# Transposing DMAs for the rounded tokens, products and bit matrices of a gated attention and feed-forward layer, a VectorE addition of bias and maximum, and a new order

## The chip, the cores and the metric

The kernel runs on one core of one Trainium2 chip. The metric is the device time of one execution in microseconds (us); the number quoted for a kernel is the median of its runs.

## What is computed

The input is 8 batches of 512 tokens with 256 features. Cut to what matters:

```python
x = x + tanh(g_xattn) * xattn(layernorm(x), ctx)      # windowed attention-free layer + MLP
x = x + tanh(g_ffn) * ffn(layernorm(x))               # ternary weights, 8-bit activations

def xattn(x, pos):                       # T=512, D=256, H=1024
    emb = x + pos
    q, k, v = emb @ wq + bq, emb @ wk + bk, emb @ wv + bv
    ek = exp(k - max(k, axis=1)); ew = exp(w - max(w, axis=1))    # w = pos_bias within 64 tokens
    y = sigmoid(q) * (ew @ (ek * v)) / (ew @ ek)
    a = layer_norm(y @ wo + bo + emb, gamma, beta)
    return layer_norm(relu(a @ w1 + b1) @ w2 + b2 + a, gamma, beta)

def act_quant(x):  scale = 127 / max(abs(x)) per token; return round(x * scale) / scale
def weight_quant(w): scale = 1 / mean(abs(w)); return clip(round(w * scale), -1, 1) / scale
def bitlinear(x, w): return act_quant(x) @ weight_quant(w).T
def ffn(x): return bitlinear(silu(bitlinear(x, w_gate)) * bitlinear(x, w_up), w_down)
```

## The kernel before

**Tiling.** A batch is four tiles of 128 tokens. Matrix products in single precision are made of three matmuls each (upper by upper, upper by lower, lower by upper half of the operands, helper `product` of the matmuls, L2342). The matmuls of the ternary feed-forward part (`gate`, `up`, `down`) are one bf16 matmul each, since rounded tokens (up to 127) and weights (-1, 0, 1) fit in bf16.

**Stages of a batch.** `emb_rows` (transposes of x + pos), `keys_T` and `key_max`/`max_row` (maximum of the keys over the tokens), `queries`, `keys_values` (k and v of a tile in one bank of 512 columns, `kv`), `attend` and `attend_far`, `project`, `n1_rows`, `hidden`, `feed_forward`, then the ternary part. Eight batches overlap: while batch b is in its keys and attention, batch b-1 is in `hidden` and `feed_forward`, and batch b-3 (later b-2) is in the ternary part.

**Keys and values.** The bias of k less the maximum, and the bias of v, are split in an upper and a lower row (`bias_parts` on VectorE, L1529 to L1534) and added by a matmul of a matrix of ones with `bias_row` (L2393), ahead of the six matmuls of the tile. ScalarE takes `exp` of k in place (L783) and copies v out (`copy_values`, L789); VectorE multiplies (`weighted`, L1541); ScalarE and VectorE split the result (`e_upper` L796, `e_lower` L1546).

**Rounding and transposing.** Tokens are rounded by adding a large number (`token_quantise`, L834), so that the rounded value lies in the low half of each 32-bit word. TensorE transposes these halves as f16 into PSUM (`xq_rows`, L2480, four transposes for two tiles), and ScalarE turns them into bf16 (`xq_columns`, L853). The products of a tile, 128 x 1024, go the same way: `product` on VectorE (L1625), its absolute maximum and scale (`product_scale`, L1631 to L1643), rounding on GpSimd for even tiles (L492) and on ScalarE for odd ones (L867), eight transposes (`hq_rows`, L2507), `hq_columns` on ScalarE (L874), `down` (L2515), `output` on VectorE (L1649). The three weight matrices, rounded once at the start, go through `bit_rows` (L2339, 16 transposes each) and `bit_columns` (L747).

**What sets the order.** Each engine has a list of steps written out by hand in its block, and does them strictly in that order. A step begins with its waits on semaphores. SyncE's list holds the DMAs, in order too: an entry that waits holds back those behind it. The table `BANK` says in which of the eight PSUM banks each step of each batch writes, and `bank_wait` lets TensorE wait for the last reader of the bank's earlier content.

Of the kernel before, what the change touches and what calls it, by code (L numbers as in the profile page):

```python
# [23 lines left out]
LIFT = ROUND + 16896.0  # L24
LIFT_SCALE, LIFT_BASE = 512.0, 1536.0
# [12 lines left out]
    ("embT", 0): (4, 3, 0, 5, 0, 3, 5, 1), ("embT", 1): (5, 6, 1, 3, 3, 5, 1, 3), ("kT", 0): (4, 5, 6, 5, 0, 3, 5, 1),  # L38
# [3 lines left out]
    ("num", 0): (1, 1, 4, 7, 6, 6, 6, 3), ("den", 0): (2, 5, 3, 3, 5, 1, 3, 5), ("num", 1): (0, 6, 1, 4, 0, 3, 5, 0),  # L42
# [5 lines left out]
    ("xqT", 0): (2, 5, 1, 2, 4, 2, 7, 3), ("xqT", 1): (2, 0, 3, 5, 1, 2, 1, 6), ("gate", 0): (4, 4, 0, 2, 4, 2, 6, 2),  # L48
    ("up", 0): (0, 6, 6, 6, 6, 2, 0, 6), ("hqT", 0): (2, 0, 3, 5, 3, 6, 0, 0), ("down", 0): (4, 0, 3, 5, 3, 6, 0, 0),
    ("gate", 1): (4, 4, 0, 2, 4, 2, 6, 2), ("up", 1): (4, 4, 0, 2, 4, 4, 0, 0), ("hqT", 1): (5, 3, 5, 1, 1, 7, 2, 1),  # L50
# [3 lines left out]
    ("down", 3): (0, 3, 5, 1, 6, 6, 3, 0)}  # L54
PAIRED = ("gate", "up")
EWT_BANKS = (0, 1, 2, 3)
TOTAL_BANKS = (0, 3, 7)
BIT_BANKS = ((5, 4), (7, 3), (2, 5))
B1_BANK = 1

# [11 lines left out]
def flamingo_layer(nc, x, ctx_in, g_xattn, g_ffn, wq, bq, wk, bk, wv, bv, wo, bo, pos_bias, gamma, beta,  # L72
                   w1, b1, w2, b2, w_gate, w_up, w_down, out):
    with ExitStack() as stack:
# [594 lines left out]
        def _(act):  # L669
# [2468 lines left out]
```

## Time and profile before

| | |
|---|---|
| median of 3 runs | 554.49 us (552.69 to 555.13) |
| profiled execution, its own time | 555.27 us |
| span of the profile | 553.5 us |
| TensorE busy | 505.9 us, 91% |
| VectorE busy | 426.3 us, 77% |
| ScalarE busy | 380.0 us, 69% |
| GpSimd busy | 245.2 us, 44% |

The profile calls the engines PE (TensorE matmul), PEld (weight load), DVE (VectorE), ACT (ScalarE), POOL (GpSimd) and SP (SyncE; SPq are the DMAs that it issues). Lines as L2507 are lines of the kernel. The rows hold only the operation, so a helper's line stands for all who call it: all three-part products are L2348. A matmul's duration in a row includes its way through the array; matmuls overlap, so that the time that one costs is the distance of its start to the next one's start.

### The profile page before, as it was taken

How to read it: one execution, taken by the hardware profiler on the slowest of the kernel's cores; microseconds unless marked ns; L12 is line 12 of the kernel's file. 1: busy time of each engine (PE TensorE's matmuls, PEld its weight loads, DVE VectorE, ACT ScalarE, POOL GpSimd, SP SyncE). 2: the span in 40 equal slices, each digit the busy share in tenths (PEclk: the TensorE clock that was granted, in tenths of full speed). 3: DMA queues.
4: the chain of work that ended last, by engine and by line, in shares of the span. 5: the costliest groups of instructions: out<-in, count | busy, mean ns of one | idle time of the engine just before them, and what ended most of it. 6: DMA issues, size and time to landing. Idle time of an engine off the chain costs nothing.

```text
span 553.5 us, 10265 instructions
## 1 busy us (share of the span) xinstructions
PE 505.9 (91%) x3270; PEld 412.3 (74%) x3270; DVE 426.3 (77%) x974; ACT 380.0 (69%) x627; POOL 245.2 (44%) x384
## 2 busy tenths in 40 slices
PE   0389999999999999999999999999999999999474
PEld 0378788988877887788877897788778877877332
DVE  3883997766899769976999679975988688858564
ACT  2667866648576877697667877677658866877474
POOL 3654106229512870359223951277114922547410
PEclk9998999999999999999999999999999999999588
DMA  7835001101200211011200120012001100010101
GB/s 258 259 92 190 2 0 39 40 1 38 77 2 1 78 40 39 1 40 38 78 1 12 67 76 2 1 46 70 1 2 39 40 0 1 14 62 5 37 3 38
DMA packets 25608, 25.31 MB, mean 46 GB/s; under 512 B 3538, under 2 KB 24532, under 8 KB 25556
## 3 DMA queue, kind: packets, MB, share of 16 engines
q1 hardware_dynamic: 24720, 24.65, 14.0%
q8 instruction: 28, 0.46, 0.4%
q14 instruction: 24, 0.20, 0.1%
q10 hardware_dynamic: 836, 0.01, 0.1%
HBM read 20.46 MB, written 4.19 MB: 45 GB/s over the span
## 4 chain that ended last, share of the span: by engine, by line
PE 82%; DVE 6%; issue 3%; ACT 3%; POOL 2%; DMA 2%; SPq 1%; ACTq 1%; POOLq 0%; DVEq 0%
PE ps L2348 53%; PE ps L2488 10%; PE ps L2515 5%; PE ps L2507 3%; PE ps L2417 3%; PE ps L2393 1%; PE ps L2365 1%; PE ps L2442 1%; ACT hqT L874 1%; PE ps L2425 1%; DVE ps L1555 1%; DMA bkv_row<-in_L_xattn_bv_dram 1%; PE ps L2356 1%; DMA x_in<-in_x_dram 1%; PE ps L2318 1%
## 5 line engine op out<-in xcount | busy, mean ns | idle before, releaser
L436 POOL TENSOR_TENSOR mv<-mv,cols 128x2 f32<-128x2 f32 x64 | 12.6, 197 | 169.1 <-DVE mv L1504 169.1
L822 ACT ACTIVATE h_hi<-ps,cols 128x512 fp32r<-128x512 f32 x64 | 44.0, 690 | 51.6 <-PE ps L2348 51.3
L2348 PE MATMUL ps<-w_hi,h_hi 128*128 128x256 f32 x256 | 74.9, 292 | 0.0
L2348 PE MATMUL ps<-w_hi,h_lo 128*128 128x256 f32 x256 | 71.4, 279 | 0.0
L2348 PE MATMUL ps<-w_lo,h_hi 128*128 128x256 f32 x256 | 71.4, 279 | 0.0
L874 ACT ACTIVATE hqT<-ps,cols 128x1024 bf16<-128x1024 f16 x32 | 35.6, 1113 | 32.0 <-PE ps L2507 31.9
L1555 DVE RECIPROCAL ps<-ps 128x512 f32<-128x512 f32 x16 | 53.7, 3359 | 4.3 <-PE ps L2425 4.3
L2348 PE MATMUL ps<-n1T_hi,w_hi 128*128 128x512 f32 x128 | 52.2, 408 | 1.1 <-DVE y_lo L1572 1.0
L1590 DVE TENSOR_TENSOR h_lo<-ps,h_hi 128x512 fp32r<-128x512 f32 x64 | 42.7, 684 | 12.6 <-ACT ps L827 12.3
L2348 PE MATMUL ps<-n1T_hi,w_lo 128*128 128x512 f32 x128 | 50.6, 395 | 0.0
L2348 PE MATMUL ps<-n1T_lo,w_hi 128*128 128x512 f32 x128 | 50.5, 394 | 0.0
L2348 PEld LDWEIGHTS ps<-w_hi,h_hi 128*128 128x128 f32 x256 | 48.1, 188 | 1.4
L2348 PEld LDWEIGHTS ps<-w_lo,h_hi 128*128 128x128 f32 x256 | 48.2, 188 | 0.8
L2348 PEld LDWEIGHTS ps<-w_hi,h_lo 128*128 128x128 f32 x256 | 48.1, 188 | 0.0
L1625 DVE TENSOR_TENSOR work<-work,ps 128x1024 f32<-128x1024 f32 x32 | 38.7, 1210 | 9.4 <-ACT work L862 6.2
L439 POOL TENSOR_TENSOR rstd<-mv,cols 128x2 f32<-128x2 f32 x64 | 44.5, 696 | 0.0
L862 ACT ACTIVATE work<-ps,cols 128x1024 f32<-128x1024 f32 x32 | 35.6, 1113 | 11.6 <-PE ps L2488 10.8
L2515 PE MATMUL ps<-wdT,hqT 128*128 128x256 bf16 x256 | 35.9, 286 | 7.9 <-ACT hqT L874 7.9
L827 ACT ACTIVATE ps<-ps,cols 128x512 f32<-128x512 f32 x64 | 42.1, 658 | 0.0
L1496 DVE BATCH_NORM_STATS2 st<-work 128x6 f32<-128x256 f32 x96 | 36.3, 414 | 3.8 <-POOL work L486 3.5
L1631 DVE TENSOR_REDUCE cols<-work 128x1 f32<-128x1024 f32 x32 | 38.7, 1210 | 0.4
L2348 PE MATMUL ps<-ew_hi,e_hi 128*128 128x256 f32 x128 | 37.7, 295 | 0.9 <-DVE e_lo L1546 0.7
(180 smaller groups left out, 1508.2 us busy)
## 6 DMA issues: line engine op xcount, KB each, us to landing
x_in<-in_x_dram SPq DMA_DIRECT2D x16, 256.0 KB, 2.9
emb<-in_ctx_dram SPq DMA_DIRECT2D x16, 256.0 KB, 3.0
work<-in_x_dram SPq DMA_DIRECT2D x8, 512.0 KB, 3.7
out_dram<-work SPq DMA_DIRECT2D x16, 256.0 KB, 2.1
work<-in_L_xattn_w_dram SPq DMA_DIRECT2D x2, 1024.0 KB, 10.0
place_c<-in_L_xattn_pos_bias_dram SPq DMA_DIRECT2D x1, 1024.0 KB, 7.4
work<-in_L_ffn_w_gate_dram SPq DMA_DIRECT2D x1, 1024.0 KB, 5.7
work<-in_L_ffn_w_up_dram SPq DMA_DIRECT2D x1, 1024.0 KB, 6.2
```

The source lines that it names most:

```text
L439: pool.tensor_tensor(rstd[:, n, c], mv[:, n, c, 1], minus_half[:, c], ALU.pow).then_inc(rstd_ok[n].sem, 1)
L822: nc.scalar.activation(h_hi[:, m % RING, :], bank(b, "h", m), ACT.Relu, bias=b1_col[:, m:m + 1]).then_inc(h_hi_ok.sem, 1)
L827: nc.scalar.activation(bank(b, "h", m), bank(b, "h", m), ACT.Relu, bias=b1_col[:, m:m + 1]).then_inc(h_relu_ok.sem, 1)
L874: nc.scalar.activation(hqT[:], bank_h(b, "hqT", t).rearrange("p (k n) -> p k n", n=P), ACT.Identity, bias=unlift_col, scale=LIFT_SCALE).th ...
L1496: nc.vector.bn_stats(st6[:, n, t, :], src[:, t, :]).then_inc(stats[n].sem, 1)
L1555: nc.vector.reciprocal(bank(b, "den", h), bank(b, "den", h)).then_inc(rden_ok.sem, 1)
L1590: nc.vector.tensor_tensor(h_lo[:, m % RING, :], bank(b, "h", m), h_hi[:, m % RING, :], ALU.subtract).then_inc(h_lo_ok.sem, 1)
L1625: nc.vector.tensor_tensor(prod[t % 2].rearrange("p (a n) -> p a n", a=2), sg.rearrange("p (a n) -> p a n", a=2), bank_pair(b, "up", t), AL ...
L1631: nc.vector.tensor_reduce(hm[:, t:t + 1], prod[t % 2], AX.X, ALU.max, apply_absolute_value=True).then_inc(hm_ok.sem, 1)
L2348: last = nc.tensor.matmul(dst, lhsT, rhs, start=(i == 0 and not begun), stop=(i == n - 1 and ends))
L2488: last = nc.tensor.matmul(dst[:, c, :], xqT[:, k, t * P:(t + 1) * P], w[:, k, c * T:(c + 1) * T], start=(k == 0), stop=(k == ND - 1))
L2515: last = nc.tensor.matmul(bank(b, "down", t)[:, 0:D], hqT[:, k, :], wdT[:, k, :], start=(k == 0), stop=(k == NH - 1))
```

## The change

**Transposes.** `xq_rows`, `hq_rows` and `bit_rows` leave TensorE's list. In their place stand DMAs that transpose 2-byte elements from SBUF to SBUF, issued by SyncE. Their source has to be bf16, so ScalarE first writes the rounded values as bf16 (`xq_whole`, `hq_whole`, `bit_whole`); the steps `xq_columns`, `hq_columns` and `bit_columns` go. `hqT` has two buffers in place of one. `gate`, `up` and `down` read their weights from blocks of 128 columns with a gap between.

**Keys and values.** `max_row` has the row of maxima in all partitions; VectorE subtracts it from the bias in one operation (`bias`) and adds the whole bias to each tile of k and v in one (`add_bias`), which also moves them to SBUF. The ones matmul, `bias_parts` and `copy_values` go, and `keys_values` no longer waits for the maximum.

**Order.** All lists, and the table of banks, are new. Start: the weights of keys and values are loaded second and split first. End: the maximum of the last batch's first tokens stands ahead of `output(6, 3)` on VectorE, and `output(7, 0)` ahead of `product(7, 3)`.

```diff
+            def xq_rows(b, p):
+                wait(sp, xq_ok, b, p + 1)
+                wait(sp, g_ps, b, 2 * p - 2)
+                wait(sp, u_ps, b, 2 * p - 2)
+                sp.dma_start_transpose(xqT[:, 2 * p:2 * p + 2, :, :], half(xq, p)).then_inc(xqT_ok[p].sem, 16)
+            def hq_rows(b, t):
+                wait(sp, hq_ok, b, t + 1)
+                sp.wait_ge(bitT_ok, 48)
+                wait(sp, d_ps, b, t - 1)
+                sp.dma_start_transpose(hqT[t % 2], hq[t % 2]).then_inc(hqT_ok[t % 2].sem, 16)
...
-                nc.scalar.activation(v_f[:, t % 2, :], bank(b, "kv", t)[:, D:2 * D], ACT.Copy).then_inc(v_ok.sem, 1)
+                nc.scalar.activation(bank(b, "kv", t)[:, 0:D], kv_f[:, t % 2, 0:D], ACT.Exp).then_inc(ek_ok.sem, 1)
...
+            def xq_whole(b, p):
+                wait(act, xr_ok, b, p + 1)
+                wait(act, xqT_ok[p], b - 1, 16)
+                nc.scalar.activation(half(xq, p), half(n3, p), ACT.Identity, bias=unlift_col).then_inc(xq_ok.sem, 1)
...
+            def hq_whole(b, t):
+                c, n = rounded_of(t)
+                wait(act, c, b, n)
+                act.wait_ge(bit_ok, 3)
+                wait(act, hqT_ok[t % 2], b, 16 * (t // 2))
+                nc.scalar.activation(hq[t % 2], prod[t % 2], ACT.Identity, bias=unlift_col).then_inc(hq_ok.sem, 1)
...
+            def bias(b):
+                wait(dve, mrow_ps, b, 1)
+                wait(dve, kvb_ok, b, 0)
+                nc.vector.tensor_tensor(bias_all[:, 0:D], bk_all[:], bank(b, "mx")[:, 0:D], ALU.subtract).then_inc(bias_ok.sem, 1)
+            def add_bias(b, t):
+                wait(dve, kv_ps, b, t + 1)
+                wait(dve, bias_ok, b, 1)
+                wait(dve, ekv_ok, b, t - 1)
+                nc.vector.tensor_tensor(kv_f[:, t % 2, :], bank(b, "kv", t), bias_all[:], ALU.add).then_inc(kvb_ok.sem, 1)
...
-                nc.tensor.matmul(dst, ones_r[:], bias_row[:], start=True, stop=False)
...
-                        last = nc.tensor.matmul(dst[:, c, :], xqT[:, k, t * P:(t + 1) * P], w[:, k, c * T:(c + 1) * T],
+                        last = nc.tensor.matmul(dst[:, c, :].rearrange("p (j n) -> p j n", n=P), xqT[:, t, k, :], w[:].rearrange("p (j k) n -> p j k n", k=ND)[:, 4 * c:4 * c + 4, k, :],
...
-                    last = nc.tensor.transpose(bank_h(b, "hqT", t)[:, k * P:(k + 1) * P], hq_h[t % 2][:, k * P:(k + 1) * P], ident_h[:])
```

TensorE's order between the second tile's `down` of batch 2 and the keys and values of batch 5; before:

```order
L2348 MATMUL ps<-wkv_hi,embT_lo 128x512
L2515 MATMUL ps<-wdT,hqT 128x256 x8
L2507 MATMUL ps<-ident_h,work 128x128 x8
L2393 MATMUL ps<-bias_row,ones_r 128x512
L2348 MATMUL ps<-wkv_hi,embT_hi 128x512
```

and now:

```order
L2365 MATMUL ps<-wkv_hi,embT_lo 128x512
L2512 MATMUL ps<-wdT,w_bit 128x256 x8
L2365 MATMUL ps<-wkv_hi,embT_hi 128x512
L2365 MATMUL ps<-wkv_lo,embT_hi 128x512
L2365 MATMUL ps<-wkv_hi,embT_lo 128x512
```

The eight transposes and the bias matmul between `down` and the tile's six matmuls are gone; `w_bit` holds the transposed products.

VectorE's order at the first product of batch 2 (`product`, bias of batch 5, `product_scale`, `first_residual` of batch 4), before:

```order
L1625 TENSOR_TENSOR work<-work,ps 128x1024
L1529 TENSOR_TENSOR ps<-bkv_row,ps 1x256
L1532 CAST bias_row<-ps 1x256
L1534 TENSOR_TENSOR bias_row<-ps,bias_row 1x256
L1631 TENSOR_REDUCE cols<-work 128x1
L1635 TENSOR_SCALAR cols<-cols 128x1
```

and now:

```order
L1628 TENSOR_TENSOR work<-work,ps 128x1024
L1531 TENSOR_TENSOR bias_all<-bk_all,ps 128x256
L1634 TENSOR_REDUCE cols<-work 128x1
L1638 TENSOR_SCALAR cols<-cols 128x1
L1641 RECIPROCAL cols<-cols 128x1
```

Three operations on one row have become one on 128 partitions, ahead of the maximum of the product.

SyncE's DMAs from batch 5's context to the reload of batch 4's x (`x_in` and `emb` inputs, `out_dram` stores, `work<-in_x_dram` the reload), before:

```order
L282 DMA emb<-in_ctx_1024_dram 128x2x256 x2
L276 DMA x_in<-in_x_dram 128x2x256 x2
L291 DMA out_dram<-work 128x2x256 x2
L287 DMA work<-in_x_dram 128x4x256
L282 DMA emb<-in_ctx_1024_dram 128x2x256 x2
```

and now:

```order
L267 DMA emb<-in_ctx_1024_dram 128x2x256 x2
L290 DMA_TRANSPOSE xqT<-xq 128x4x128 x2
L261 DMA x_in<-in_x_dram 128x2x256 x2
L297 DMA_TRANSPOSE w_bit<-place_c 128x8x128 x3
L276 DMA out_dram<-work 128x2x256
L297 DMA_TRANSPOSE w_bit<-place_c 128x8x128
L276 DMA out_dram<-work 128x2x256
```

Six transposing DMAs of a batch stand in the same queue as its loads and stores: the loads of x wait behind those of the tokens, the stores behind those of the products.

## Rows read from the trace of the kernel before

**Rows 1.** The page: busy time of each engine, share of the span, instructions.

```profile
PE 505.9 (91%) x3270; PEld 412.3 (74%) x3270; DVE 426.3 (77%) x974; ACT 380.0 (69%) x627; POOL 245.2 (44%) x384
```

**Rows 2.** Windows: one batch, the full stretch, the end; busy us, granted clock.

```profile
236.60:297.00 60.40, 60.33 (x399) 49.31 (x398) 49.76 (x117) 44.35 (x76) 28.94 (x46) 1.00 0.12 36
120.20:506.10 385.90, 384.12 (x2526) 314.69 (x2524) 311.29 (x719) 280.20 (x474) 184.56 (x283) 1.00 0.10 31
506.10:553.50 47.40, 28.69 (x178) 15.79 (x176) 28.44 (x74) 26.99 (x36) 13.55 (x26) 0.77 0.07 23
```

**Rows 3.** Timeline of TensorE: start us, us; eight transposes, bias matmul, next matmuls.

```profile
302.48 0.61 PE L2507 MATMUL ps<-ident_h,work 128*128 128x128 f16 x8
302.90 0.48 PE L2393 MATMUL ps<-bias_row,ones_r 128*128 128x512 f32 x1
303.21 0.39 PE L2348 MATMUL ps<-wkv_hi,embT_hi 128*128 128x512 f32 x1
```

**Rows 4.** Chain that ended last, in order of time: start us, us, what.

```profile
463.44 1.41 PE ps L2348 x12
...
465.31 0.86 PE ps L2488 x4
...
504.17 0.46 PE ps L2507 x8
504.63 0.22 PE ps L2480 x4
```

**Rows 5.** Timeline of TensorE: transposes of the first weight matrix.

```profile
41.06 1.87 PE L2339 MATMUL ps<-ident_h,work 128*128 128x128 f16 x16
42.68 0.78 PE L2393 MATMUL ps<-bias_row,ones_r 128*128 128x512 f32 x1
```

**Rows 6.** Groups of VectorE: xcount | busy us, mean ns | idle before.

```profile
L1590 DVE TENSOR_TENSOR h_lo<-ps,h_hi 128x512 fp32r<-128x512 f32 x64 | 42.7, 684 | 12.6 <-ACT ps L827 12.3
...
L1529 DVE TENSOR_TENSOR ps<-bkv_row,ps 1x256 f32<-1x256 f32 x8 | 3.3, 409 | 0.8 <-PE ps L2382 0.8
```

**Rows 7.** Groups of ScalarE, same columns.

```profile
L874 ACT ACTIVATE hqT<-ps,cols 128x1024 bf16<-128x1024 f16 x32 | 35.6, 1113 | 32.0 <-PE ps L2507 31.9
...
L867 ACT ACTIVATE work<-work,cols 128x1024 f32<-128x1024 f32 x16 | 19.8, 1238 | 4.0 <-DVE cols L1640 4.0
```

**Rows 8.** DMA issues: xcount, KB each, median us from issue to landing.

```profile
x_in<-in_x_dram SPq DMA_DIRECT2D x16, 256.0 KB, 2.9
...
out_dram<-work SPq DMA_DIRECT2D x16, 256.0 KB, 2.1
...
vecs<-in_L_xattn_b_dram SPq DMA_DIRECT2D x1, 128.0 KB, 4.8
```

**Rows 9.** Timeline of TensorE: end of first up, eight transposes, first down, batch 2.

```profile
282.00 0.61 PE L2382 MATMUL ps<-ident,cols 128*128 128x128 f32 x4
...
288.05 0.62 PE L2507 MATMUL ps<-ident_h,work 128*128 128x128 f16 x8
...
291.94 1.04 PE L2515 MATMUL ps<-wdT,hqT 128*128 128x256 bf16 x8
```

**Rows 10.** Timeline of GpSimd: rounding of that tile's products.

```profile
286.88 1.11 POOL L492 TENSOR_SCALAR work<-work,cols 128x1024 f32<-128x1024 f32 x1
```

**Rows 11.** Chain, the end: tokens of batch 7, its last tile.

```profile
526.63 0.62 PE ps L2480 x4
...
527.27 0.70 ACT xqT L853
...
528.21 3.44 PE ps L2488 x8
...
547.27 1.12 ACT hqT L874
...
548.53 1.88 PE ps L2515 x8
```

**Rows 12.** Timeline of ScalarE: upper half of the key and value weights.

```profile
28.17 1.05 ACT L683 ACTIVATE wkv_hi<-work 128x1024 fp32r<-128x1024 f32 x1
```

More of the change, by code:

```diff
@@ L1330, in _ @@
             silu(5, 1)
-            hq_columns(5, 0)
+            hq_whole(5, 0)
             normalise_tile(7, 0)
@@ L2268, in _ @@
             tile_stats(7, 2, 3)
-            output(6, 0)
+            product(6, 2)
             mean_variance(7, 2, 1)
-            product(6, 2)
             product_scale(6, 2)
             product(6, 3)
+            output(6, 0)
             output(6, 1)
@@ L2602, in _ @@
             hidden(0, 3)
+            feed_forward(0, 0)
+            feed_forward(0, 1)
+            emb_rows(2, 0)
             hidden(0, 4)
@@ L2605, in _ @@
             hidden(0, 6)
-            hidden(0, 7)
-            feed_forward(0, 0)
-            feed_forward(0, 1)
             feed_forward(0, 2)
             feed_forward(0, 3)
+            hidden(0, 7)
             project(1, 0)
@@ L2660, in _ @@
             attend(2, "num", 1, 3)
+            feed_forward(1, 2)
+            attend_far(2, "den", 0)
+            attend_far(2, "den", 1)
+            attend(2, "num", 0, 1)
+            attend(2, "num", 0, 2)
+            attend(2, "num", 0, 3)
+            attend_far(2, "num", 0)
             attend_far(2, "num", 1)
@@ L2670, in _ @@
             feed_forward(1, 4)
+            feed_forward(1, 5)
+            gate(0, 0)
             keys_T(3, 0)
             keys_T(3, 1)
-            queries(3, 0)
-            gate(0, 0)
-            queries(3, 1)
             up(0, 0)
+            gate(0, 1)
             max_row(3)
-            gate(0, 1)
             project(2, 0)
@@ L2745, in _ @@
             keys_T(4, 1)
-            queries(4, 0)
+            feed_forward(2, 5)
             gate(1, 0)
-            queries(4, 1)
             up(1, 0)
@@ L2818, in _ @@
             keys_T(5, 1)
-            queries(5, 0)
+            feed_forward(3, 5)
             gate(2, 0)
-            queries(5, 1)
             up(2, 0)
@@ L2883, in _ @@
             hidden(4, 5)
+            hidden(4, 6)
             feed_forward(4, 3)
-            hidden(4, 6)
             hidden(4, 7)
             emb_rows(6, 0)
+            project(5, 0)
+            project(5, 1)
+            project(5, 2)
+            project(5, 3)
+            gate(3, 0)
+            up(3, 0)
             emb_rows(6, 1)
@@ L2952, in _ @@
             attend(6, "num", 1, 3)
+            attend_far(6, "den", 0)
+            feed_forward(5, 2)
+            attend_far(6, "den", 1)
+            attend(6, "num", 0, 1)
+            attend(6, "num", 0, 2)
+            attend(6, "num", 0, 3)
+            attend_far(6, "num", 0)
             attend_far(6, "num", 1)
@@ L2956, in _ @@
             hidden(5, 5)
+            hidden(5, 6)
             feed_forward(5, 3)
-            hidden(5, 6)
+            gate(4, 0)
             hidden(5, 7)
+            up(4, 0)
+            gate(4, 1)
+            project(6, 0)
+            gate(4, 2)
+            project(6, 1)
+            project(6, 2)
+            project(6, 3)
+            up(4, 1)
             emb_rows(7, 0)
@@ L2981, in _ @@
             down(4, 0)
+            max_row(7)
             feed_forward(5, 6)
             gate(4, 3)
-            hq_rows(4, 1)
+            queries(7, 0)
+            queries(7, 1)
+            down(4, 1)
             feed_half(5)
```

1797 lines of the change are left out of this document (846 added, 951 removed), and 16 rows, old and new, of the table BANK.

## The prediction

> **What bounds the kernel now.** I read the page's busy times first, then the windows, then the chain of waits. TensorE is busy 91% of the span, VectorE 77%, ScalarE 69% [rows 1]. The windows say where the missing 9% of TensorE is: from 120.2 to 506.1 us it is busy 384.1 of 385.9 us at a granted clock of 1.00, while VectorE is busy 311.3 us in the same stretch [rows 2]. So for 386 us the kernel is as long as TensorE's list, and whatever leaves that list there leaves the time. The other two parts differ: a start of some 68 us, where loads and the first chain set the pace, and an end of 47.4 us, where TensorE is busy 28.7 us at a mean clock of 0.77 [rows 2] and the chain goes from engine to engine. There an operation of TensorE counts only as one link of a chain, and so does what replaces it. The profiled execution took 555.27 us for a span of 553.5 us, 0.8 us above the median; I sum on the span and carry the difference over.
>
> **What leaves TensorE.** A matmul costs the distance to the next start. The bias matmul of 512 columns: its start to the next one's is 0.31 us in the row shown, of which 0.08 us come from the change of type after the transposes, so 0.23 us, and 32 x 0.23 = 7.4 us; all lie ahead of 506 us. Eight transposes of products cost 0.42 us on the timeline [rows 3] and 0.46 us on the chain [rows 4]; 24 of the 32 groups (batches 0 to 5) and the first of batch 6 lie ahead of 506 us: 25 x 0.44 = 11.0 us. Four transposes of tokens cost 0.22 us [rows 4]; 14 of 16 groups lie ahead: 3.1 us. The three weight matrices: the first costs 1.6 us (41.06 to 42.68 us, before the clock rose) [rows 5], the others I count at twice the 0.44 us of eight, 0.9 us each: 3.4 us. Together 24.9 us. Of the single batch that I looked at, 60.4 us long [rows 2], this takes 4 x 0.23 + 4 x 0.44 + 2 x 0.22 = 3.1 us, which makes 57.3 us.
>
> **What VectorE takes over.** `add_bias` moves 128 x 512 from PSUM; the nearest row, a subtraction of that size from PSUM, has 0.684 us, and the three one-row operations that go have 0.41 us each, one like them staying [rows 6]. Per batch 4 x 0.68 - 3 x 0.41 + 0.41 = +1.9 us: VectorE goes from 49.8 us of 60.4 (82%) to 51.7 of 57.3 (90%). What hides it is that VectorE works for other batches ahead of need; TensorE's three `hidden` after the keys and values are its cover. If that cover failed altogether, each of the 4 x 0.68 us would be a stall of TensorE: 2.7 us a batch, 18 us over some 6.5 batches. If it holds, 0. I take 2.5 us in all, near the lower end, since 5.6 us of VectorE's batch stay free. ScalarE loses the copy of v and reads the products from SBUF (1.24 us as its rounding there, against 1.11 us from PSUM) [rows 7]: nearly even, no new bound.
>
> **The transposing DMA, the unknown.** No row shows one. Call L the time from the ready bf16 to the landed transpose of 128 x 1024 (256 KB). The nearest rows are plain DMAs: a store of 256 KB out of SBUF 2.1 us, a load into SBUF 2.9 us, and 4.8 us for a 128 KB one that stood behind others [rows 8]. I take 3 us, by the load of the same size, and keep 2.1 and 5 us as bounds; that transposing could cost more is a rival below. What does the new order leave for L? In the batch shown, `up` of the first tile ends at 282.0 us and its `down` starts at 291.94 us, 9.9 us later [rows 9]; the new list puts both `queries` between (12 matmuls at 0.23 us, 2.8 us) and takes a `feed_forward` (12 matmuls of 256 columns, 1.4 us), one `up` (0.9 us) and the transposes (0.5 us) out [rows 4], so the distance stays at 9.9 us. The rounding ended at 286.88 + 1.11 = 288.0 us, 6.0 us after `up` [rows 10]; with two one-row operations less ahead of it on VectorE it is 5.2 us. `hq_whole` adds 1.24 us and a hand-over 0.1 us: 6.5 us. So 3.4 us are left for L, and by the same count about 3.4 us for the third tile; the second has about 4.4 us, the fourth more than 8. With L = 3 nothing waits. Above 3.4 us each of the first and third tile stalls TensorE by the excess, twice a batch. The tokens' transposes have more than 10 us. Behind a waiting transpose on SyncE stand the loads of x and the stores; x is needed two batches later, so they have room.
>
> **The Trainium skill on this.** The page "VectorE: DVE Perf Modes", section "The three transpose paths", gives 1309 ns for one 128 x 128 transpose by DMA against 390 ns on TensorE, and advises TensorE where PSUM will do. This trace has 0.46 us for eight on TensorE in a row, far below that figure, and nothing for the DMA. The page "Advanced Engine Details and Errata", section "X-Bar Transpose (TRN2)", says that they are as fast as regular DMAs, which is the assumption of the sum above; the first, taken eight times in a row, would be L = 10.5 us, an estimate from that page, and by it the kernel would be far slower.
>
> **Start.** The split of the key and value weights (1.05 us) stands at 28.17 us between the two halves of the embedding on ScalarE, with TensorE waiting for the second [rows 12]; it moves ahead into idle time: -1.0 us. The order of the loads shifts the rest by up to 1 us either way.
>
> **End.** Three places get longer by the DMA. Tokens of batch 7: now 0.62 us of transposes and 0.70 us of columns, 1.6 us from 526.63 to 528.21 us [rows 11]; then some 0.7 us for `xq_whole` plus L plus 0.1 us = 3.8 us: +2.2. The last tile: rounding ended at 546.03 us (544.80 + 1.24, the mean of its row), `down` started at 548.53 us, 2.5 us [rows 7, 11]; then 1.24 + 3 + 0.1 = 4.3 us: +1.8. `output(7, 0)` now stands ahead of `product(7, 3)` on VectorE and waits for a first tile that is later by L: about +1.5. Against this, the maximum of batch 7's first tokens no longer stands behind `output(6, 3)`: -1.1. End: +4.4 us, and 3 us more for each us of L.
>
> **The sum.** 553.5 - 24.9 - 1.0 + 2.5 + 4.4 = 534.5 us of span; with the 1.8 us around it 536.3, less 0.8 us to the median: 535.5 us.
>
> **The rivals.** (a) L between 3.4 and 4.5 us, partly uncovered. At 4 us: 0.6 us x 2 x 6.5 batches = 8 us in the full stretch, 3 us at the end: 546.5 us. For it: a transposing DMA can hardly be quicker than a plain one. Against: the plain ones here are below 3.4 us. (b) Slower than before: the transposes are the bound. At L = 5 us it is 1.6 x 2 x 6.5 = 21 us and 6 us at the end: 562 us. The place is the first and third `down` of each batch; it decides from L = 4.5 us on, where 1.1 x 13 + 4.5 = 19 us cancel the forecast's gain of 19 us. By the skill's 1309 ns eight times over, this case would be the one, with 7.1 x 13 + 22 = 114 us, some 650 us. For it: many small pieces make a DMA slow, as the 4.8 us of 128 KB hint. (c) VectorE becomes the bound: it is 90% full, and its list waits at other places than before. At the full 18 us in place of my 2.5 us: 551 us. Against: even now it waits over 10 us a batch without holding TensorE up. (d) The gapped weights of `gate` and `up` stream slower; no row shows such an operand. Double time would be 256 x 0.22 = 56 us; nothing speaks for it, 2 in 100, kept in (b)'s share.
>
> **Chances.** Forecast (L up to 3.4 us, cover holds) 0.50; (a) 0.20; (c) 0.12; (b) with (d) 0.18. A measurement of this kernel tells about 0.5% (2.8 us) from no change. Faster: 0.50 + 0.20 + half of (c) and a little less = 0.76; same: 0.06, from the edges of (b) and (c); slower 0.18. The low end: L = 2.1 us gives -2.7 at the end, full cover -2.5, the start -1 more: 529; with stalls of TensorE in the first 120 us that a better order could take away, 525 us. The high end is (c) whole and (b) at its mild end, 556 us. Outside lie the rest of (b) and little else, under 2 in 10.
>
> **What would show it.** TensorE's window between two batches' keys and values at 57 to 58 us and still over 99% busy; transposing DMAs landing 2.5 to 3.4 us after issue; VectorE at about 52 us a batch; no wait of a `down` matmul for a DMA in the full stretch, and such waits of 2 us and more at the end. Wrong, if the window is 60 us or more: with idle time ahead of `down` it is (b) or (a); with waits of the attention matmuls for VectorE's lower halves it is (c); with TensorE's `gate` matmuls above 0.22 us apart it is (d).

## The result and the profile after

The changed kernel takes 538.47 us (median of 4 runs, 534.96 to 538.88) against 554.32 us for the kernel before in the same session: a ratio of 0.970, 95% interval 0.966 to 0.975. It is faster by 15.9 us; the forecast was 19. The profiled execution took 538.58 us for a span of 536.8 us, and I compare spans. Two executions of the experiments below, one of 1236.8 us in extra_512 and one of 552.47 us in late_bits, lie apart from the others of their kernels, and the medians given are those of the others.

The page after; engine, busy us, share of the span, instructions, against [rows 1]:

```profile
PE 476.4 (89%) x2870; PEld 386.4 (72%) x2870; DVE 432.5 (81%) x984; ACT 375.3 (70%) x592; POOL 246.3 (46%) x384
```

TensorE's busy time fell by 29.5 us, the span by 16.7: TensorE now idles 12.8 us more. The windows say where. Their columns are the stretch, its length, busy us of PE, PEld, DVE, ACT and POOL, then granted clock, DMA share and GB/s; the fourth row is one batch, from its first `add_bias` to the next batch's, the last is the end:

```profile
0.00:41.50 41.50, 15.68 (x78) 13.99 (x78) 23.45 (x58) 21.85 (x29) 20.82 (x33) 0.88 0.74 218
41.50:122.80 81.30, 74.61 (x447) 64.35 (x447) 62.88 (x129) 48.62 (x78) 27.34 (x46) 0.98 0.24 61
122.80:234.40 111.60, 110.31 (x685) 91.11 (x684) 97.98 (x227) 84.96 (x140) 57.43 (x90) 1.00 0.21 54
234.40:291.85 57.45, 56.44 (x355) 46.54 (x353) 50.94 (x120) 43.88 (x72) 29.16 (x46) 1.00 0.28 61
291.85:353.97 62.12, 60.09 (x367) 49.48 (x365) 54.14 (x128) 45.97 (x74) 29.07 (x46) 0.97 0.24 62
...
486.60:536.80 50.20, 27.25 (x113) 12.13 (x112) 29.68 (x79) 27.41 (x36) 13.52 (x26) 0.68 0.34 69
```

A batch takes 57.45 us against 60.40 [rows 2]. Ahead of the end TensorE's busy time fell by 28.1 us (477.2 us up to 506.1 before, 449.2 up to 486.6 now). Part of this did not come out as time: TensorE idles 5.4 us more in the first 122.8 us (32.5 us against 27.1 before) and 3.2 us more in the stretch behind (4.9 us against 1.8 [rows 2]). The end, behind the last matmul of `feed_forward`, is 50.2 us against 47.4. So -28.1 + 5.4 + 3.2 + 2.8 = -16.7 us.

TensorE's waits from 19 us, behind its first, to the end of the stretch; us in total, times, longest:

```profile
PE ps L2373 <- POOL emb L504: 5.4, 1, 5.4
PE ps L2365 <- DVE embT_lo L1510: 3.2, 1, 3.2
PE ps L2365 <- DVE y_lo L1575: 2.0, 2, 1.7
PE ps L2365 <- DVE e_lo L1549: 1.7, 1, 1.7
PE ps L2382 <- ACT embT_hi L823: 1.6, 2, 1.1
...
PE ps L2512 <- DMA w_bit<-place_c: 0.3, 1, 0.3
```

Two more groups, small ones, recur from batch to batch. In the one batch from 225.92 us (its first `down`) to 283.36 us TensorE waits twice for VectorE, ahead of the transposes of the embedding:

```profile
PE ps L2373 <- DVE h_lo L1593: 0.6, 1, 0.6
PE ps L2373 <- DVE y_lo L1575: 0.3, 1, 0.3
```

`down` waits for a transposing DMA 0.3 us in all before the end, and 14.2 us in the end. What the DMA takes from issue to landing, over the stretch from 120 to 486 us:

```profile
w_bit<-place_c SPq DMA_TRANSPOSE x24, 3.1
xqT<-xq SPq DMA_TRANSPOSE x14, 2.7
```

How close this is, the four tiles of batch 2 show. ScalarE writes the bf16 products (start us, us):

```profile
278.76 1.15 ACT L920 ACTIVATE place_c<-work,cols 128x1024 bf16<-128x1024 f32 x1 [1.35 <-POOL work L549]
285.56 1.14 ACT L920 ACTIVATE place_c<-work,cols 128x1024 bf16<-128x1024 f32 x1
288.81 1.15 ACT L920 ACTIVATE place_c<-work,cols 128x1024 bf16<-128x1024 f32 x1
296.03 1.15 ACT L920 ACTIVATE place_c<-work,cols 128x1024 bf16<-128x1024 f32 x1
```

and TensorE starts the four `down`, never idle before them:

```profile
283.36 0.38 PE L2512 MATMUL ps<-wdT,w_bit 128*128 128x256 bf16 x2
291.07 0.39 PE L2512 MATMUL ps<-wdT,w_bit 128*128 128x256 bf16 x2
293.35 0.39 PE L2512 MATMUL ps<-wdT,w_bit 128*128 128x256 bf16 x2
301.32 0.39 PE L2512 MATMUL ps<-wdT,w_bit 128*128 128x256 bf16 x2
```

From the end of each write to the start of its `down` are 3.4, 4.4, 3.4 and 4.1 us, and the DMA needs 3.1. For the first and the third tile 0.3 us are to spare.

### The profile page after: what moved, and what is told of

The parts are those of the page before. It is cut to its first block, busy times and chain, and to the rows that moved or that the text cites. A ratio compares the mean times of both kernels' runs of the same rounds, so it can differ in the third digit from the quotient of the medians.

```text
span 536.8 us, 9468 instructions
## 1 busy us (share of the span) xinstructions
PE 476.4 (89%) x2870; PEld 386.4 (72%) x2870; DVE 432.5 (81%) x984; ACT 375.3 (70%) x592; POOL 246.3 (46%) x384
## 4 chain that ended last, share of the span: by engine, by line
PE 69%; DVE 14%; DMA 6%; ACT 5%; issue 4%; POOL 1%; SPq 0%; DVEq 0%; ACTq 0%; POOLq 0%
PE ps L2365 47%; PE ps L2493 9%; DVE ps L1558 5%; PE ps L2512 5%; PE ps L2431 3%; DMA work<-in_L_xattn_w_dram 2%; DMA w_bit<-place_c 2%; DVE cols L1634 2%; PE ps L2382 1%; DVE ps L1571 1%; PE ps L2456 1%; PE ps L2373 1%; DVE work L1628 1%; DMA wuT<-w_bit 1%; PE ps L2439 1%
## 5 line engine op out<-in xcount | busy, mean ns | idle before, releaser
L869 ACT ACTIVATE h_hi<-ps,cols 128x512 fp32r<-128x512 f32 x64 | 44.3, 692 | 29.5 <-PE ps L2365 27.5
L2512 PE MATMUL ps<-wdT,w_bit 128*128 128x256 bf16 x256 | 38.3, 300 | 14.5 <-DMA w_bit<-place_c 14.5
L920 ACT ACTIVATE place_c<-work,cols 128x1024 bf16<-128x1024 f32 x32 | 36.7, 1147 | 14.7 <-POOL work L549 14.1
L2512 PEld LDWEIGHTS ps<-wdT,w_bit 128*128 128x128 bf16 x256 | 24.7, 105 | 28.3 <-DMA w_bit<-place_c 20.2
L809 ACT ACTIVATE work<-work,nmr,rstd 128x256 f32<-128x256 f32 x64 | 34.8, 599 | 12.6 <-POOL nmr L499 12.4
L2493 PE MATMUL ps<-wgT,xqT 128*128 128x512 bf16 x128 | 34.5, 395 | 5.6 <-DMA xqT<-xq 5.2
```

The source lines that it names most:

```text
L809: last = nc.scalar.activation(dst[:, t, :], src[:, t, :], ACT.Identity, bias=nmr[:, n, t:t + 1], scale=rstd[:, n, t:t + 1])
L869: nc.scalar.activation(h_hi[:, m % RING, :], bank(b, "h", m), ACT.Relu, bias=b1_col[:, m:m + 1]).then_inc(h_hi_ok.sem, 1)
L920: nc.scalar.activation(hq[t % 2], prod[t % 2], ACT.Identity, bias=unlift_col).then_inc(hq_ok.sem, 1)
L2493: last = nc.tensor.matmul(dst[:, c, :].rearrange("p (j n) -> p j n", n=P), xqT[:, t, k, :], w[:].rearrange("p (j k) n -> p j k n", k=ND)[: ...
L2512: last = nc.tensor.matmul(bank(b, "down", t)[:, 0:D].rearrange("p (k n) -> p k n", n=P), hqT[t % 2][:, k, :], wdT[:].rearrange("p (k j) n ...
```

## The experiments

All are edits of the changed kernel, and all compute the whole layer. "More" and "less" are differences of medians to its 538.47 us; kernels of other sessions stand against it with an uncertainty of some 2.5 us, so where less is at stake I look at marks in the traces, above all the start of the first `down` of batch 0 (168.44 us) and the last `down` (531.71 us). These marks scatter too: in end_busy, which changes nothing ahead of the first of them, it stands at 171.97 us, since the start alone took longer.

**Is TensorE's list still the bound?** One more matmul of 512 columns per product of keys and values, and eight more of 128 columns per `down`:

```diff
+                nc.tensor.matmul(dst, tile_ones[:, 0:P], wkv_hi[:, 0, :], start=True, stop=True)
                 product(dst, [...])
```

> The changed kernel with one more matmul of 512 columns ahead of each product of keys and values, into the same bank, which the product then overwrites: what the bias matmul cost TensorE, put back while VectorE still adds the bias. My theory: TensorE's list is still the bound, so 32 times 0.23 us, 7.4 us more (6 to 8). Rival (VectorE or a transposing DMA has become the bound, so the shorter list bought nothing at this place): 0 to 3 us more.

543.85 us, 5.4 more (6 to 8 were expected; the difference is within what sessions differ by), and a batch takes 58.26 us against 57.44: 0.21 us for each.

```diff
+                for k in range(NH):
+                    nc.tensor.matmul(bank(b, "down", t)[:, (k % 4) * P:(k % 4 + 1) * P], hqT[t % 2][:, k, :], wdT[:, k, :],
+                                     start=True, stop=True)
```

> The changed kernel with eight more matmuls of 128 columns in bf16 ahead of each `down`, into the bank that it then overwrites: about what the eight transposes of a product took of TensorE's list, at a place where they wait for the transposing DMA as `down` does. My theory: 0.42 to 0.46 us each 32 times, 13.4 to 14.7 us more. Rival (the pace is VectorE's or the DMA's): under 8 us. Together with extra_512 it says how much of the gain is the shorter list of TensorE.

551.83 us, 13.4 more, and a batch takes 59.14 us: 0.43 us for each eight. So the two groups cost about what the forecast took them for, and putting them back costs 18.8 us, against the 28.1 us that the list lost in all; tokens and weights, forecast at 6.5 us, were not tried. TensorE's list is still a bound, and both rivals fall; the next experiment shows that it is not the only one.

**How much room has VectorE?** `add_bias` twice:

```diff
                 nc.vector.tensor_tensor(kv_f[:, t % 2, :], bank(b, "kv", t), bias_all[:], ALU.add).then_inc(kvb_ok.sem, 1)
+                wait(dve, kvb_ok, b, 2 * t + 1)
+                nc.vector.tensor_tensor(kv_f[:, t % 2, :], bank(b, "kv", t), bias_all[:], ALU.add).then_inc(kvb_ok.sem, 1)
```

> The changed kernel, `add_bias` done twice, the second after the first (0.68 us each, 32 more, 21.8 us of VectorE's time); nothing is left out. My theory: VectorE has 6 us a batch free in the full stretch, so most is hidden; it costs where VectorE is late already (55 to 85 us, 320 to 330 us), and in each batch less than the whole: 3 to 9 us more. Rival (VectorE is the bound of the changed kernel in the full stretch): 20 us more or over. Other rival (wholly hidden): within 1 us.

559.33 us, 20.9 more for 21.8 us of added work: the rival. A batch, from its first `down` to the next one's, takes 59.69 us, 2.25 more for four additions of 0.68 us, though VectorE idles 6 us in it:

```profile
236.46:296.15 59.69, 57.28 (x353) 46.50 (x352) 53.50 (x122) 43.95 (x72) 29.13 (x46) 1.00 0.22 58
```

and TensorE waits ten times for what comes last of the keys and values; in the changed kernel it does so once, at 80 us:

```profile
PE ps L2368 <- DVE e_lo L1552: 10.5, 10, 1.9
```

The ten waits are half of the 20.9 us; how the rest divides is open. So the share of busy time misled me when I wrote this expectation. A second bound is a chain (product, `add_bias`, exponential, `weighted`, rounding, `e_lower`) that is nearly as long as what TensorE has to do meanwhile. By these numbers some 0.5 us a batch is left in it (2.7 us added, 2.25 paid), and the two traces show the place. In the changed kernel the second `e_lower` of batch 5, of 0.69 us, ends at 301.35 us, 0.8 us before the first `attend`:

```profile
300.66 0.69 DVE L1549 TENSOR_TENSOR e_lo<-ps,e_hi 128x512 fp32r<-128x512 f32 x1
302.12 0.36 PE L2365 MATMUL ps<-ew_hi,e_hi 128*128 128x256 f32 x1
```

and in bias_twice TensorE waits 0.89 us for it:

```profile
316.37 0.68 DVE L1552 TENSOR_TENSOR e_lo<-ps,e_hi 128x512 fp32r<-128x512 f32 x1
317.19 0.36 PE L2368 MATMUL ps<-ew_hi,e_hi 128*128 128x256 f32 x1 [0.89 <-DVE e_lo L1552]
```

This `attend` takes only the first tile's values. It waits for the second `e_lower` because it writes that tile's bank: `BANK` gives `num` 1 and `kv` 1 of batch 5 the same bank, 6 (those of batches 3 and 4 share one as well). So at this place the table of banks sets the room, not the data; no run tries another bank.

**How much room has the transposing DMA?** Each product transposed twice, one after the other:

```diff
                 sp.dma_start_transpose(hqT[t % 2], hq[t % 2]).then_inc(hqT_ok[t % 2].sem, 16)
+                wait(sp, hqT_ok[t % 2], b, 32 * (t // 2) + 16)
+                sp.dma_start_transpose(hqT[t % 2], hq[t % 2]).then_inc(hqT_ok[t % 2].sem, 16)
```

> The changed kernel, each product transpose issued a second time after the first has landed, so that L, the time from the ready bf16 product to its landed transpose, goes from 3.1 to about 6.2 us; all else is the same and nothing is left out. My theory: the room ahead of the first and the third `down` of a batch is 3.4 us, so each of these stalls TensorE by 2.8 to 2.9 us, 13 times, 37 us, and the end grows by three times 3.1 us, 9 us: 585 us against 538.5. Rival (the trace hides more room, or TensorE has other work to do meanwhile): under 20 us more. Second rival (every stall adds up, the second and fourth `down` too, which had 4.4 and 4.1 us): 1.9 + 2.1 us more per batch, 26 us on top, 611 us.

600.72 us, 62 more, between theory and second rival. The waits of TensorE and the batch from its first `down` to the next one's:

```profile
PE ps L2514 <- DMA w_bit<-place_c: 63.2, 24, 7.4
```

```profile
237.99:302.91 64.92, 58.41 (x352) 47.38 (x353) 51.10 (x118) 44.33 (x73) 29.13 (x46) 0.97 0.29 70
```

This batch grows by 7.5 us, not 5.8 (the five from the first `down` of batch 0 to that of batch 5 by 4.9 to 8.1): the second and the fourth tile are pressed too, and TensorE's clock is 0.97. The end, behind the last `down` of batch 5, grows from 66.1 to 83.1 us: 17 us, 5.5 times the 3.1 us that were added, not 3 times.

The tokens transposed twice, by the same edit in `xq_rows`:

```diff
                 sp.dma_start_transpose(xqT[:, 2 * p:2 * p + 2, :, :], half(xq, p)).then_inc(xqT_ok[p].sem, 16)
+                wait(sp, xqT_ok[p], b, 16)
+                sp.dma_start_transpose(xqT[:, 2 * p:2 * p + 2, :, :], half(xq, p)).then_inc(xqT_ok[p].sem, 16)
```

> The changed kernel, each token transpose (128 KB) issued a second time after the first has landed: 2.4 us more from the ready tokens to their landed transpose. My theory: in the full stretch the tokens have over 10 us of room, so nothing there; in the end the first tokens of batch 7 lie on the chain and some of the second: 2.4 to 5 us more, 541 to 543.5 us. Rival (SyncE's queue or the DMA engines are short, so that any transposing DMA costs its time wherever it stands): 16 times 2.4 us, 38 us more.

548.6 us, 10 more. A batch of the full stretch takes 57.47 us, as in the changed kernel (57.44): the added 2.4 us are hidden there, as forecast, and neither queue nor DMA engines are short. The time arises in the end, where TensorE waits for tokens four times; in the changed kernel it does so twice, for 5.2 us:

```profile
PE ps L2495 <- DMA xqT<-xq: 15.8, 4, 6.0
```

All four token transposes of batches 6 and 7 lie on the chain there, 4 x 2.4 = 9.6 us; I had counted one or two. The trace is that of the slowest of ten executions, 554.32 us: from the last `down` of batch 5 it shows 78.1 us against 66.1, and the other 4 us of it lie ahead of the first `down` of batch 0, at 172.56 us, about where end_busy has it.

**The start.** The changed kernel's first transposes of the embedding come at 28.75 us, the kernel before has them at 26.53. That is more than scatter: in the eight other traces with the same start they come at 28.88 to 30.78 us. I first blamed the order of loads, and put w2 back ahead of the key and value weights:

```diff
-            fetch_wkv()
             fetch_w2()
+            fetch_wkv()
...
-            wkv_upper()
             w2_upper()
+            wkv_upper()
...
-            wkv_lower()
             position_max()
+            wkv_lower()
```

> The changed kernel with w2 again loaded and rounded ahead of the key and value weights, and the maximum of the positions ahead of their lower half on VectorE. My theory: the changed load order made the start later (TensorE's first instruction at 19.95 us against 18.31 before, the first transposes of the embedding at 28.75 against 26.53), since ScalarE waits for w2 until 15.45 us with the exponentials behind it and GpSimd's 4.5 us for w2 delay the first normalisation. So TensorE starts at 17 to 18.5 us, the embedding's transposes come 1.5 to 2.8 us earlier, and the time is 1 to 2.5 us lower: 536 to 537.5. Rival (the first keys and values wait for something else, the vectors' load or VectorE, and the earlier start is lost by 45 us): within 0.5 us of 538.5.

539.39 us: no gain, near the rival's number, but for neither reason. w2 still lands at 15.5 us, and the embedding's transposes start at 30.98 us. VectorE's subtraction for the key and value weights (1.21 us in the kernel before) now runs beside GpSimd's for w2, though how much of the 2.2 us this makes is open, as end_busy has the transposes at 30.78 us without it:

```profile
18.44 4.72 DVE L1420 TENSOR_TENSOR wkv_lo<-work,wkv_hi 128x1024 fp32r<-128x1024 f32 x1 [3.88 <-ACT wkv_hi L740]
```

```profile
17.54 4.54 POOL L483 TENSOR_TENSOR w_lo<-work,w_hi 128x2048 fp32r<-128x2048 f32 x1 [5.68 <-ACT w_hi L766]
```

More of the same kind, without its diff here (x ahead of ctx, `mean_variance` ahead of the lower halves, the gate matrix's total behind the queries) built on that order:

> As loads_back, and more: x of batch 0 is loaded ahead of the query and output weights and of ctx, both `mean_variance` of batch 0 stand ahead of the lower halves of wq and wo, and what prepares the gate matrix (its total on TensorE, its magnitudes on ScalarE) stands behind the first keys and queries. My theory: the embedding's transposes start at 23 to 25 us in place of 28.75, the first keys and values at 37 to 39 us in place of 41.5, and the time falls by 3 to 5 us: 533.5 to 535.5. Rival (VectorE, which is busy without a gap from 54 to 70 us, takes it back): 1 us or less.

541.38 us, no gain; the transposes start at 29.83 us behind the same 4.72 us subtraction. The answer stood in the rates of the DMA engines, in GB/s, 1.25 us each, of the first 50 us. Before:

```profile
GB/s 0 15 105 211 392 283 301 370 362 384 409 363 352 223 10 96 319 369 325 360 210 231 200 101 65 37 210 0 7 24 342 53 13 20 189 372 331 402 398 334
```

The changed kernel:

```profile
GB/s 0 7 115 231 406 287 311 240 160 206 331 373 356 349 374 341 272 49 70 292 379 310 365 208 51 178 249 0 0 212 214 32 215 173 94 346 363 400 409 302
```

From the eighth to the tenth number 240, 160, 206 stand against 370, 362, 384: 0.64 MB less in 3.75 us. What is new there are the loads of bk and bv into 128 partitions, 128 KB each, on ScalarE's queue. Put behind w1 on SyncE's:

```diff
-            vector("vectors1", bk_all[:], bk[None, :].to_broadcast([P, D]))
-            vector("vectors1", bias_all[:, D:2 * D], bv[None, :].to_broadcast([P, D]))
...
             fetch_w1()
+            fetch_rows()
             fetch_gate()
```

> The changed kernel with its two new loads of bk and bv into all 128 partitions (128 KB each) taken from the front of ScalarE's queue and put behind w1 on SyncE's. My theory, new after loads_back: it is not the order that made the start late. In the trace of the changed kernel and of loads_back the DMA engines move 145 to 250 GB/s from 8 to 13 us, where the kernel before moves 300 to 380; what is new there are these two loads in small packets. So w2 lands at 11.5 to 13 us in place of 15.4, TensorE starts at 17.5 to 18.5 us in place of 19.95, the embedding's transposes at 26 to 27.5 in place of 28.75, and the time falls by 1.5 to 2.5 us: 536 to 537. Rival (the slump has another cause, such as the key and value weights' 512 KB at the front): w2 still lands at 15 us, no change in the time.

535.68 us (6 runs, 535.24 to 538.35), ratio to before 0.969 (0.967 to 0.972). The rates:

```profile
GB/s 0 5 115 233 408 277 291 373 359 348 348 347 370 413 379 134 84 255 377 300 368 247 51 98 312 20 0 65 333 29 157 211 175 313 378 408 397 269 118 105
```

TensorE's timeline, its first transposes and those of the embedding:

```profile
17.95 3.65 PE L2344 MATMUL ps<-ident,place_c 128*128 128x128 f32 x16 [17.95 <-ACT place_c L775]
26.34 1.97 PE L2377 MATMUL ps<-ident,emb 128*128 128x128 f32 x8 [4.74 <-POOL emb L509]
```

The slump is gone, w2 is there at 13.0 us, and everything behind is earlier by 2.4 us (embedding), 2.6 us (first `down`, at 165.89) and 2.8 us (last `down`, at 528.92). late_bits below, with the same loads, repeats it (w2 at 12.9 us, embedding at 26.29), and in all eleven traces with the two loads in front w2 lands at 15.4 to 17.4 us. The theory holds for the start; the edit changes both the time and the queue of the two loads, and which of the two counts is not told apart. By the medians it beats the changed kernel by 2.8 us, against the kernel before of its own session it gains 17.2 us for the changed kernel's 15.9; the two ratios alone would leave room for no gain.

**TensorE's waits for VectorE.** The changed kernel loses 3.2 us at 60 us and 1.7 us at 80 and 324 us. At 324 us VectorE's list, in a row without a gap, is two reciprocals and what stands between them and `y_lower(5, 1)`, the last line, for which TensorE waits:

```profile
315.17 3.36 DVE L1558 RECIPROCAL ps<-ps 128x512 f32<-128x512 f32 x1
...
319.62 3.36 DVE L1558 RECIPROCAL ps<-ps 128x512 f32<-128x512 f32 x1
322.89 0.68 DVE L1575 TENSOR_TENSOR y_lo<-ps,y_hi 128x512 fp32r<-128x512 f32 x1
323.48 0.69 DVE L1571 TENSOR_TENSOR ps<-ps,work 128x512 f32<-128x512 f32 x1
324.07 1.07 DVE L1497 BATCH_NORM_STATS2 st<-x_in 128x6 f32<-128x256 f32 x3
...
325.23 0.69 DVE L1575 TENSOR_TENSOR y_lo<-ps,y_hi 128x512 fp32r<-128x512 f32 x1
```

I tried three times to order this better, and lost each time. Of the first, vector_order, the moves on VectorE's list in part:

```diff
             gated(0, 0)
+            emb_lower(1, 0)
+            gated(0, 1)
+            emb_lower(1, 1)
             inverse(0, 0)
-            gated(0, 1)
             divided(0, 0)
...
+            y_lower(5, 1)
+            emb_lower(6, 0)
             tile_stats(7, 0, 0)
...
             mean_variance(7, 0, 0)
-            y_lower(5, 1)
-            emb_lower(6, 0)
```

> The changed kernel with another order of VectorE's and ScalarE's lists at three places: the lower halves of batch 1's embedding ahead of the first reciprocal, and clipping a weight matrix behind `y_lower(0, 1)`; the rounding of the last bit matrix, which waits 2.5 us for a transposing DMA at 75 us, behind the exponentials of batch 1; the statistics of x of batch 7 behind `y_lower(5, 1)`. My theory: TensorE's waits of 3.2, 1.7 and 1.7 us for VectorE at 60, 80 and 324 us shrink by 1.5 us or more each, and what the lower clock after the last one cost goes with it: 4 to 6 us less, 532.5 to 534.5. Rival (VectorE's own list is the bound in the first 120 us, so a wait only moves): 1.5 to 2 us less, from the place at 324 us alone.

551.35 us, 12.9 more. Two of TensorE's lines, at the second queries of batch 1 and at its first keys and values:

```profile
69.49 0.77 PE L2365 MATMUL ps<-embT_hi,wq_hi 128*128 128x512 f32 x1 [8.09 <-DVE y_lo L1575]
77.15 0.76 PE L2365 MATMUL ps<-wkv_hi,embT_hi 128*128 128x512 f32 x1 [3.91 <-ACT work L830]
```

The embedding's lower halves were in time, but `queries(1, 1)` writes the bank of the first denominator, which `y_lower(0, 0)` reads last, and that came later with the reciprocal. ScalarE, next, waited 11.2 us for a normalisation whose statistics I had moved behind `bias(1)`, which waits for TensorE. The move at 324 us changed nothing: without the statistics ahead of it `y_lower(5, 1)` waits 1.06 us for ScalarE, and TensorE as long as before. The second, small_orders; the diff is the first of its three moves:

```diff
             emb_rows(6, 0)
+            gate(3, 0)
             project(5, 0)
...
-            gate(3, 0)
             up(3, 0)
```

> The changed kernel with three small moves: the first `gate` of batch 3 stands ahead of `project(5, 0)` on TensorE, into its wait of 1.7 us for VectorE at 324 us; the rounding of the last bit matrix, which makes ScalarE wait for a transposing DMA at 76 us, stands behind the exponentials and upper halves of batch 1; and `product(7, 3)` stands ahead of `output(7, 0)` on VectorE. My theory: 1.7 us and some 1 us of lower clock go at the first place, 1.3 us at the second, 0.4 us at the third: 3 to 4.5 us less, 534 to 535.5. Rival (VectorE or ScalarE is the bound around the first two places, so the waits only move, as in vector_order): 0 to 1 us less.

542.1 us, 3.6 more. `gate(3, 0)` was no filler: it writes bank 4, whose last reader is `hidden_lower(4, 6)`, and that stands behind the reciprocals as well.

```profile
PE ps L2493 <- DVE h_lo L1593: 4.1, 1, 4.1
```

The first `down` of batch 3 is 3.3 us later than in the changed kernel, 0.6 us of it from the start; at 80 us the wait was 0.4 us, but so it was in loads_back, start_order and rows_later, which leave that place alone, so the second move shows nothing. The third attempt, late_bits, builds on rows_later and moved the second and third bit matrix's clipping, rounding and transposing DMAs away from batch 1:

The main lines, on SyncE and VectorE:

```diff
+            fetch_ctx(2, 0)
+            fetch_ctx(2, 1)
             bit_rows(1)
-            bit_rows(2)
-            fetch_ctx(2, 0)
-            fetch_ctx(2, 1)
             fetch_x(3, 0)
             fetch_x(3, 1)
+            bit_rows(2)
...
             inverse(0, 0)
+            emb_lower(1, 0)
+            emb_lower(1, 1)
```

> As rows_later, and in the first 120 us what rounds the second and third bit matrix (needed by TensorE from 156 us on) is moved out of the way of batches 0 and 1: clipping them on VectorE behind `e_lower(1, 1)` and `e_lower(1, 3)`, rounding and storing them on ScalarE behind the upper halves of batch 1, their transposing DMAs behind the loads of ctx of batch 2; the lower halves of batch 1's embedding stand directly behind the first reciprocal, not ahead of it as in vector_order; and `product(7, 3)` stands ahead of `output(7, 0)`. My theory: the first queries of batch 1 start at 59.5 to 60.5 us in place of 62.0, `y_lower(0, 1)` 1.2 us earlier, the first `down` of batch 0 1.5 to 2.5 us earlier than the 165.9 us of rows_later: 533 to 534.5 us. Rival (the two reciprocals and the chain of the division on VectorE hold the pace there, and everything else is off it): within 0.7 us of rows_later's 535.7. Worse rival (as in vector_order, a list in order puts something behind a later wait): 538 or more.

547.46 us, 11.8 more than rows_later. The first queries of batch 1 did start earlier, at 59.97 us for 62.00, but ScalarE's list then met the queue of SyncE:

```profile
97.15 2.00 ACT L802 ACTIVATE w_bit<-place_c,cols 128x2048 bf16<-128x2048 f32 x1 [9.58 <-DMA wuT<-w_bit]
```

```profile
102.52 0.55 PE L2369 MATMUL ps<-w_hi,h_hi 128*128 128x256 f32 x1 [7.31 <-DVE h_lo L1597]
```

The transpose of the up matrix waited on SyncE behind the load of ctx of batch 2, which finds its buffer free only at 90.9 us; the third bit matrix needs the buffer that this transpose reads, and behind it on ScalarE stood the hidden layer. "Needed from 156 us on" was true of TensorE, not of what is queued behind.

**The end's clock.** TensorE runs at a mean clock of 0.68 in the end. 39 matmuls fill its waits there:

```diff
+            def keep_busy(dst, n):
+                for i in range(n):
+                    nc.tensor.matmul(dst, wgT[:, 0, :], wdT[:, 0:4, :], start=True, stop=True)
```

> The changed kernel with 39 more matmuls of 512 columns in the last 45 us, in TensorE's waits for a transposing DMA, into banks that the next step overwrites; their number is chosen to end before the DMA lands. My theory: the end costs more than the DMA's own time, since TensorE falls to the lower clock in each of these waits (1.89 us for a `down` against 1.05, 1.9 for a `gate` against 1.02); with the clock held the chain gets shorter by 0.8 us at three or four `down` and two `gate`: 3 to 5 us less, 533.5 to 535.5. Rival (the chain of the end runs through VectorE, ScalarE and the DMA, and TensorE's clock hardly counts): less than 1 us. If the fill is too long or does not raise the clock: no gain or a loss.

539.99 us, no gain. The clock did rise, in a window of the same stretch as the 0.68:

```profile
488.80:538.10 49.30, 29.52 (x149) 13.53 (x151) 29.61 (x78) 27.41 (x35) 13.53 (x26) 0.95 0.35 70
```

From the last `down` of batch 5 the trace shows 65.3 us against 66.1. Even these 0.8 us are not the clock's: loads_back, start_order and small_orders have 65.4, 65.3 and 65.3 us there without the fill, at a clock of 0.70 to 0.76 in the same window. The chain of the end runs through the other engines and the DMA, as the rival said.

## Why the prediction was right, and where not

**TensorE's list** (24.9 us up to the end): right, and a little small, 28.1 us of busy time. extra_512 and extra_eight confirm two of its prices, 0.21 us (forecast 0.23) and 0.43 us (0.44). The 3 us beyond are not split up by any run; these two prices, both below the forecast, are not where they come from. That 0.08 us of the bias matmul's 0.31 us come from the change of type is not shown: in the changed kernel 0.30 us also stand between two matmuls behind a product of the same types (297.05 and 297.35 us).

**The batch**: 57.3 us forecast, 57.4 measured; VectorE 51.7 us forecast, 50.9 measured. The sign "still over 99% busy" failed: TensorE is busy 56.4 of 57.45 us, 98%, and waits 0.9 us for VectorE where the embedding is transposed; the batch of the kernel before has no such wait. TensorE's busy time of a batch fell by 3.9 us where 3.1 were forecast, so the two errors cancel. Rival (d) is out: the matmuls of `gate` and `up` start 0.216 us apart in both kernels.

**L**: 3 us forecast, 3.1 measured, from the plain load of the same size [rows 8]; the room was forecast at 3.4, 4.4, 3.4 and over 8 us and is 3.4, 4.4, 3.4 and 4.1, so the fourth tile was off by half, which hq_twice shows to matter. The figure of the Trainium skill by which it would have been far slower ("VectorE: DVE Perf Modes", "The three transpose paths", 1309 ns for one 128 x 128) doesn't add up over the eight of them in one DMA: 3.1 us against the 10.5 us that I had estimated from that page. The other rule of the Trainium skill ("Advanced Engine Details and Errata", "X-Bar Transpose (TRN2)", as fast as regular DMAs) agrees with the trace: 3.1 us beside 3.4 for a load of 256 KB into `x_in` and 2.2 for a store. The forecast won by 0.3 us of room, which is luck as much as working, and its slope was too flat: hq_twice shows 7.5 us a batch and 17 us in the end where I had 5.8 and 9. Spread evenly over the 2.8 us beyond 3.4 us, the 62 us of that run are 22 us for each us of L, an estimate by which rival (b) would have decided from about 4.3 us on, near my 4.5.

**VectorE** (+2.5 us, rival (c) up to 18): the stretch behind 122.8 us idles 3.2 us more, made of 1.7 us at 324 us and 2.2 us in the waits of three batches at the embedding's transposes, less what the kernel before waited, so the allowance was nearly right. The ground that I gave was wrong. I counted free time in a batch; bias_twice shows that the cover is used up but for some 0.5 us, and what it added beyond that was paid in full.

**The start** (-1.0 us): wrong in sign, 5.4 us more of idle TensorE in place of a gain. The gain itself came in part: TensorE's wait for the embedding's second half is 0.5 us against 1.05. The step that failed is "the order of the loads shifts the rest by up to 1 us either way". I had costed the moved weights and not the added loads: rows_later puts 2.5 us on bk and bv. The rest arises between 55 and 85 us, where VectorE is busy without a gap from 54 to 70 us, and ScalarE waits 2.5 us for the transposing DMA of a weight matrix. No attempt there gained, so the cause of this rest stays argued, not shown. That keys and values begin 1.1 us earlier than before (41.54 us, against 42.68 us for the bias matmul [rows 5]) fits the missing transposes of the first weight matrix, 1.6 us ahead of it, and is no sign of an earlier start.

**The end** (+4.4 us): +2.8 in the windows. The last tile was right: rounding ends at 527.38 us, `down` starts at 531.71, 4.3 us, as forecast:

```profile
526.14 1.24 ACT L911 ACTIVATE work<-work,cols 128x1024 f32<-128x1024 f32 x1 [1.09 <-DVE cols L1643]
527.41 1.15 ACT L920 ACTIVATE place_c<-work,cols 128x1024 bf16<-128x1024 f32 x1
```

For batch 7's tokens I forecast 3.8 us and it took 4.5 (504.48 to 508.93): SyncE had the transpose behind the store of batch 6, which waits for `output(6, 3)`. I had looked at what stands behind a transpose in that queue, not at what stands ahead:

```profile
505.88 0.38 SPq L276 DMA_DIRECT2D out_dram<-work  x1
506.36 1.21 SPq L290 DMA_TRANSPOSE xqT<-xq  x1
```

`output(7, 0)` ahead of `product(7, 3)` cost 0.4 us at most, not 1.5 (522.55 to 522.94 us): the product would have waited for ScalarE anyway. And xq_twice shows that the end depends on four token transposes, where the sum had one.

Altogether the span came out 2.3 us above the sum: -3.2 (list), +6.4 (start), +0.7 (VectorE), -1.6 (end). That it came so close owes something to a list that was taken too small and a start of the wrong sign.

## What to carry to other kernels

When work leaves the engine that bounds a loop for a DMA, add up the distance from the ready input to the consumer's start and compare it with the DMA's latency tile by tile: that, and not the share of busy time, tells whether it is free and how near the cliff is. Cost every load that a change adds at the front, for what it does to the others in flight, and before moving an instruction in lists that run in order ask three things of it: which buffer or bank it frees late, what stands behind its new wait, and what stands ahead of it in the queue that it depends on. A loop in which TensorE hardly waits may still have next to no room on another chain; doubling one operation shows that at once.

## What the runs showed of the hardware that I had not expected

- A transposing DMA of 256 KB in bf16, eight blocks of 128 x 128, from SBUF to SBUF lands 3.1 us after issue (3.03 to 4.68 us, 32 of them), one of 128 KB after 2.4 us in the whole kernel's median and 2.7 in the full stretch: half the size saves 0.6 us (2.40 against 3.03 us at their quickest). SyncE is held 1.2 us by issuing one.
- Two loads of 128 KB from a row into 128 partitions nearly halve what the DMA engines move for 3.75 us: 160 to 240 GB/s for 362 to 384, though both together are 0.25 MB.
- A VectorE subtraction of 128 x 1024 from SBUF takes 1.2 us alone (kernel before) and 4.7 us beside a GpSimd subtraction of 128 x 2048 (4.5 us) in loads_back and start_order; in loads_back it ends 1.1 us after GpSimd's, at 23.16 and 22.08 us.
- The same wait of 1.7 us at 324 us costs 1.5 us more in some executions than in others. From the `project` behind it to the next keys and values take 24.4 us in the changed kernel, start_order and vector_order, and 22.8 us in loads_back, rows_later and end_busy. In the first the matmuls behind the wait are 0.21 us apart in place of 0.12 for 3 us and more: TensorE's lower clock (granted 0.50 from 327 to 330 us, 1.00 at the same place in loads_back), which the window of 62.12 us above shows as 0.97.
- In the end the clock did not matter: the 66.1 us from the last `down` of batch 5 became 65.3 us with the granted clock at 0.95 in place of 0.68, and 65.3 us also in start_order, at 0.70.
